# Vision tower on one core: ScalarE issues the image loads, gray stores and gathers, and the rows of maxima go in one transfer

## What is computed

```python
gray = jnp.einsum('bchw,c->bhw', x, w)[:, None]
edges = jax.lax.conv_general_dilated(gray, scharr, (1, 1), 'SAME', ...)
edge = jnp.sqrt(jnp.square(edges)).sum(axis=1) / 2
h = concatenate([cls_tok, edge], axis=1)          # 257 tokens
h = h + attention(layernorm(h))                   # softmax, causal
h = h + ffn(layernorm(h))                         # quantised input, weights and product
```

## Time and profile before

| | us |
|---|---|
| median of 3 runs | 1346.86 (1345.83 to 1353.33) |
| the profiled execution | 1357.62 |
| its span from the first to the last instruction | 1355.9 |
| TensorE busy in it | 1036.2 (76%) |
| VectorE busy | 857.1 (63%) |
| ScalarE busy | 685.5 (51%) |
| GpSimd busy | 537.8 (40%) |

### The profile page before, as it was taken

The page is one execution under the profiler, slowest core; times in us unless marked ns, Lnnn a source line. Parts: engine busy times, 40 slices in busy tenths (PEclk is TensorE's granted clock), DMA queues, the critical chain, the costliest instruction groups (busy, mean ns, idle before and its releaser), DMA issues. The chain is left out here.

```text
span 1355.9 us, 28643 instructions
## 1 busy us (share of the span) xinstructions
PE 1036.2 (76%) x9565; PEld 711.0 (52%) x9574; DVE 857.1 (63%) x1987; ACT 685.5 (51%) x1171; POOL 537.8 (40%) x645
## 2 busy tenths in 40 slices
PE   2458888888898988988898898887743766636665
PEld 1236666666666666666666666666532333313332
DVE  2134656667666676666676755664555888888664
ACT  1235555556555555655565555544223676633332
POOL 4244554465555555555555554543210000003222
PEclk9978989899999899999999988987766999976656
DMA  3565445555455554554565544423200334401764
GB/s 102 142 136 143 109 113 126 131 128 150 111 141 132 131 131 124 150 136 127 126 147 130 135 120 109 106 61 101 68 10 1 128 138 160 170 1 48 234 233 160
DMA packets 158498, 164.38 MB, mean 121 GB/s; under 512 B 29384, under 2 KB 153196, under 8 KB 155372
## 3 DMA queue, kind: packets, MB, share of 16 engines
q1 hardware_dynamic: 158444, 163.68, 44.4%
HBM read 73.26 MB, written 34.12 MB: 79 GB/s over the span
## 5 line engine op out<-in xcount | busy, mean ns | idle before, releaser
L519 ACT ACTIVATE prob<-ST 128x772 f32<-128x772 f32 x256 | 209.6, 819 | 218.3 <-PE ST L929 215.1
L684 DVE TENSOR_REDUCE mneg<-SX 128x2 f32<-128x258 f32 x256 | 107.6, 420 | 313.6 <-PE SX L915 313.1
L912 PE MATMUL SX<-kst,qst 96*128 96x257 bf16 (+1 forms) x1024 | 168.7, 259 | 44.1 <-DMA qst<-qpart 39.4
L929 PE MATMUL ST<-qst,kst 98*128 98x256 bf16 (+2 forms) x1536 | 145.5, 229 | 45.5 <-DMA qst<-mpart 45.0
L686 DVE TENSOR_REDUCE mneg<-SX 128x2 f32<-128x514 f32 x256 | 173.9, 679 | 0.0
L929 PEld LDWEIGHTS ST<-qst,kst 98*128 98x128 bf16 x1536 | 124.6, 102 | 69.3 <-DMA qst<-mpart 32.8
L915 PE MATMUL SX<-mask_s,ident_b 128*128 128x256 bf16 x512 | 148.2, 290 | 0.0
L912 PEld LDWEIGHTS SX<-kst,qst 96*128 96x128 bf16 x1024 | 97.1, 102 | 90.0 <-issue 64.3
L445 POOL TENSOR_SCALAR_AFFINE_SELECT prob<-prob 128x1016 f32<-128x1016 f32 x128 | 142.3, 1112 | 0.0
L1512 PE MATMUL GU<-qst,hq 128*128 128x256 bf16 (+1 forms) x384 | 87.2, 379 | 49.1 <-ACT hq L1303 49.1
L948 PE MATMUL G<-prob,vaug 128*32 128x256 f32 (+2 forms) x3072 | 118.9, 285 | 2.6 <-POOL prob L445 2.5
(11 more groups left out here) (228 smaller groups left out, 2106.0 us busy)
## 6 DMA issues: line engine op xcount, KB each, us to landing
kst<-kpart SPq DMA_DIRECT2D x192, 128.5 KB, 2.5
gst<-gray_dram SPq DMA_DIRECT2D x96, 256.0 KB
qst<-qpart SPq DMA_DIRECT2D x192, 128.0 KB, 2.4
h_dram<-hb SPq DMA_DIRECT2D x12, 1280.0 KB, 4.6
hb<-h_dram SPq DMA_DIRECT2D x12, 1280.0 KB, 6.1
wg_raw<-in_x SPq DMA_DIRECT2D x48, 256.0 KB, 4.0
wu_raw<-in_x SPq DMA_DIRECT2D x48, 256.0 KB, 4.1
gray_dram<-gray SPq DMA_DIRECT2D x64, 128.0 KB, 2.8
```

The source lines that it names most:

```text
L519: nc.scalar.activation(prob[:, g % 2, 2 * (u % 2):2 * (u % 2) + 2, 0:QEND], ST[:, :, 0:QEND], ACT.Exp).then_inc(exp_done, 1)
L684: nc.vector.tensor_reduce(mneg[:, 0, u // 4, 0, at], SX[:, :, S0:S0 + P + 1], AX.X, ALU.max, negate=True)
L912: mm(SX[:, r, at:at + k], qst[par][0:SR, 2 * u + r, P * t:P * t + P], kst[par][0:SR, 2 * u + r, 0:k], start=t == 1, stop=False)
L929: last = mm(ST[0:KEYS[k], r, QAT[k]:QAT[k] + QN[k]], kst[par_][:, i, KFIRST[k]:KFIRST[k] + KEYS[k]], qst[par_][:, i, Q0[k]:IMG], start=Tru ...
```

## The change

Five things change, all in the attention block:

1. `load_x`, the gray store and the gathers leave SP for ScalarE. `images()` (loads of image n+1, then the store of `bW`) stands behind the exponential of unit 5 of `bT`. `gathers(0, GR, 0)`, the three large gathers, stands behind the exponential of unit 7 of `bT`, and `gathers(GR, 2, 3 * GR)`, the three small ones, behind that of unit 1 of `bS`. The same bytes are moved by the same number of transfers (11 per image). The load of image 0 stays on SP.
2. `max_rows` issues one transfer of 2 x 8 x 256 in place of two of 1 x 8 x 256; the waits for `m_loaded` follow.
3. On VectorE `split(bS, 0)` stands before `edge_stats(bC)`, not behind it.
4. On SP the wait for `sT_done` stands before the `vlast` transfer, which now waits for `max_done` and no longer for `v_last` and `pv_done`.
5. On SP the wait for `rec_spread` ahead of `rec` is left out.

```diff
             def max_rows(b, par, half_):
 
                 if valid(b):
                     wait(sp, msplit, b, 2, half_ + 1)
-                    for i in range(2):
-                        sp.dma_start(qst[par][SR + i:SR + i + 1, 8 * half_:8 * half_ + 8, :],
-                                     mpart[half_][8 * i:8 * i + 8, :]).then_inc(m_loaded[half_], 16)
+                    sp.dma_start(qst[par][SR:SR + 2, 8 * half_:8 * half_ + 8, :], mpart[half_][:, :]
+                                 ).then_inc(m_loaded[half_], 16)
...
                     wait(sp, rec_done, bO, 1, 1)
-                    wait(sp, rec_spread, bO - 1, 1, 1)
                     sp.dma_start(rec[:, :], den[:, :]).then_inc(rec_moved, 16)
-                if valid(bW):
-                    wait(sp, gray_step, bW, 2, 2)
-                    wait(sp, gst_loaded, bC, 96, 96)
-                    for t in range(QT):
-                        sp.dma_start(gray_dram[1 + P * t:1 + P * t + P, 1:1 + IMG],
-                                     gray[:, t, :]).then_inc(gray_saved, 16)
-                if valid(n + 1):
-                    wait(sp, gray_step, bW, 2, 2)
-                    load_x(n + 1, odd)
-                if valid(bW):
-                    wait(sp, gray_saved, bW, 32, 32)
-                    wait(sp, conv_done, bC, 2, 2)
-                    for dx in range(3):
-                        for row, k, at in ((0, GR, GR * dx), (GR, 2, 3 * GR + 2 * dx)):
...
                 max_rows(bS, par, 0)
+                wait(sp, sT_done, bT, 8, 8)
                 if valid(bS):
-                    wait(sp, v_last, bS, 1, 1)
-                    wait(sp, pv_done, bT - 1, 4, 4)
+                    wait(sp, max_done, bS, 8, 4)
...
                 if valid(bP):
-                    wait(sp, sT_done, bT, 8, 8)
                     wait(sp, k_low, bP, 1, 1)
...
+                def images():
+
+                    if valid(n + 1):
+                        wait(act, gray_step, bW, 2, 2)
+                        load_x(n + 1, odd)
+                    if valid(bW):
+                        wait(act, gray_step, bW, 2, 2)
+                        wait(act, gst_loaded, bC, 96, 96)
+                        for t in range(QT):
+                            act.dma_start(gray_dram[1 + P * t:1 + P * t + P, 1:1 + IMG],
+                                          gray[:, t, :]).then_inc(gray_saved, 16)
+
+                def gathers(row, k, first):
+
+                    if valid(bW):
+                        wait(act, gray_saved, bW, 32, 32)
+                        wait(act, conv_done, bC, 2, 2)
+                        for dx in range(3):
+                            at = first + k * dx
+                            src = bass.AP(gray_dram.tensor, dx + row * (IMG + 2),
+                                          [[IMG + 2, k], [GR * (IMG + 2), GB], [1, IMG]])
+                            act.dma_start(gst[at:at + k, :, :], src).then_inc(gst_loaded, 16)
...
                 exponential(bT, 5)
+                images()
                 queries(0)
...
                 exponential(bT, 7)
+                gathers(0, GR, 0)
...
                 exponential(bS, 1)
+                gathers(GR, 2, 3 * GR)
...
                 edge_tile(bC, 1)
+                split(bS, 0)
                 edge_stats(bC)
-                split(bS, 0)
                 maxima(bS, 4)
```

More of the change, by code:

```diff
@@ L288, in vit_tower @@
         block = attention.enter_context(nc.Block())
+        xv = x.rearrange("b c (t p) w -> b p c t w", p=P)
         @block.sync
@@ L332, in _ @@
             sp.wait_ge(s_zero, 16 * 8)
[L333 to L340, removed]
+            for c in range(CH):
+                sp.dma_start(xin[0][:, c, :, :], xv[0][:, c]).then_inc(x_loaded[0], 16)
             def max_rows(b, par, half_):
@@ L360, in step @@
                     wait(sp, rec_done, bO, 1, 1)
-                    wait(sp, rec_spread, bO - 1, 1, 1)
                     sp.dma_start(rec[:, :], den[:, :]).then_inc(rec_moved, 16)
-                if valid(bW):
-                    wait(sp, gray_step, bW, 2, 2)
-                    wait(sp, gst_loaded, bC, 96, 96)
-                    for t in range(QT):
-                        sp.dma_start(gray_dram[1 + P * t:1 + P * t + P, 1:1 + IMG],
-                                     gray[:, t, :]).then_inc(gray_saved, 16)
-                if valid(n + 1):
-                    wait(sp, gray_step, bW, 2, 2)
-                    load_x(n + 1, odd)
-                if valid(bW):
-                    wait(sp, gray_saved, bW, 32, 32)
-                    wait(sp, conv_done, bC, 2, 2)
-                    for dx in range(3):
-                        for row, k, at in ((0, GR, GR * dx), (GR, 2, 3 * GR + 2 * dx)):
-                            src = bass.AP(gray_dram.tensor, dx + row * (IMG + 2),
-                                          [[IMG + 2, k], [GR * (IMG + 2), GB], [1, IMG]])
-                            sp.dma_start(gst[at:at + k, :, :], src).then_inc(gst_loaded, 16)
                 max_rows(bS, par, 0)
+                wait(sp, sT_done, bT, 8, 8)
                 if valid(bS):
-                    wait(sp, v_last, bS, 1, 1)
-                    wait(sp, pv_done, bT - 1, 4, 4)
+                    wait(sp, max_done, bS, 8, 4)
                     sp.dma_start(vaug[par][KW - 1:KW, KT - 1, :, 0:HD], vlast[:, :].rearrange("p (h d) -> p h d", d=HD)
@@ L505, in _, with load_x @@
             act.wait_ge(s_prep, 11)
+            def load_x(b, par):
+                src = xv[b] if isinstance(b, int) else xv[bass.ds(b, 1)].rearrange("o p c t w -> (o p) c t w")
+                for c in range(CH):
+                    act.dma_start(xin[par][:, c, :, :], src[:, c]).then_inc(x_loaded[par], 16)
             def step(n, par):
-                bC, bP, bS, bT = n - 2, n - 3, n - 4, n - 5
+                bW, bC, bP, bS, bT = n - 1, n - 2, n - 3, n - 4, n - 5
+                odd = 1 - par
+                def images():
[17 more added lines that the diff above has]
+                            act.dma_start(gst[at:at + k, :, :], src).then_inc(gst_loaded, 16)
                 def exponential(b, u):
@@ L699, in split @@
                     wait(dve, mT_done, b, 2, half_ + 1)
-                    wait(dve, m_loaded[half_], b - 1, 32, 32)
+                    wait(dve, m_loaded[half_], b - 1, 16, 16)
                     nc.vector.tensor_copy(mpart[half_][:, :], M[1][0:H, 0:IMG]).then_inc(msplit, 1)
@@ L924, in scores_t @@
                         if u % 4 == 0:
-                            wait(pe, m_loaded[u // 4], b, 32, 32)
+                            wait(pe, m_loaded[u // 4], b, 16, 16)
                         for r in range(2):
```

## The result

| | us |
|---|---|
| median before, 4 runs | 1346.34 (1341.0 to 1353.33) |
| median after, 4 runs | 1436.33 (1429.3 to 1440.69) |
| ratio | 1.066, 95% interval 1.0595 to 1.0725 |
| the profiled execution of after | 1429.3 (span 1427.6) |

Slower by 90 us, 33 above the forecast and inside the range. The table of stretches of the changed kernel first (columns as in the earlier trace rows): 200 to 800 us, which answers to the earlier trace rows; the 8 us behind a `scores(0)` at 604.09 and those behind one at 237.20; the 10 us in which gathers, `kst` and `qst` move together; and five single microseconds of that meeting and of its end.

The account below looks back on a forecast made before the run. Bound: a per-image ring through TensorE, VectorE, SP and DMA. Terms -0.4 - 0.7 - 0.2 + 2.9 + 0.45 = +2.05 us per image; 28 x 2.0 = 56; 1357.6 + 56, less 10.8: 1403 us, range 1318 to 1439.

Parts of the forecast that it names:

- The landing: Last `qst` issue to `scores(0)`: late gathers meet `kst` and `qst` on the DMA engines, +2.9 us per image.
- image 0: The old trace's one meeting of gathers and `kst`: 4.81 us to `scores(0)` instead of 1.93, 193 GB/s at share 1.16.
- rival A: DMA queues fill each other's gaps, rate rising to 300 GB/s: 1311 us, or 1330 with a remainder; chance 0.25.
- B: Gains and losses cancel, `qst` landing 1.0 to 1.5 us later: 1340 to 1354 us; chance 0.12.
- The other signs: Profile after: `qst<-qpart` wait 80 us or more, `qst<-mpart` below 25, `kst` within some 1.5 us of the first gather.
- The split, the one transfer, `rec`: VectorE's earlier split, one transfer for the maxima, `rec` leaving earlier: -0.4, -0.7 and -0.2 us per image.
- Issuing: Eleven issues moved from SP to ScalarE: nothing gained on SP, zero cost taken on ScalarE, 0.5 us kept for the range.
- Rival C: SP held at each ScalarE issue, its bursts exceeding 3.84 us: about +1.3 us more per image, 1439 us; chance 0.13.
- a sign against itself: TensorE's waits for exponentials appearing where it had none would show the forecast wrong on ScalarE.
- The clock: TensorE idle about 3 us before each `scores(0)`: every image, not about half, pays 0.9 us, +0.45 us per image.
- the 28 images: Images 1 to 28 or so meet the new overlap: 28 x 2.0 = 56 us; nothing taken for head and tail.
- the ring: Each image's chain: about 15.7 us from `scores(0)` to SP's rows of maxima, then 12 us of SP and DMA.

Follow-up runs that it names:

- e5: Changed kernel with each gather moving one of its eight blocks, same issues, places and engines: 1300.56 us.
- e7: Kernel before with parts 2 to 5 of the change, SP issuing all, its six gathers moved between `vlast` and `kst`: 1474.03 us.
- e10: Changed kernel with twenty useless products on TensorE in the wait for the stacked queries: 1361.36 us.
- e11: Kernel before with six useless products on TensorE in the wait for the stacked queries: 1328.58 us.
- e1: Changed kernel with ScalarE's loads, store and gathers issued earlier, some 3 us further ahead of `kst`: 1341.93 us.
- e2: Kernel before with parts 2 to 5 of the change, SP still issuing loads, store and gathers: 1292.15 us.
- e3: Changed kernel with two transfers for the rows of maxima and the split behind the statistics, as before: 1408.48 us.

## Why the prediction was right, and what it mis-sized

**The landing: right.** 1.98 became 4.68, +2.70 for the +2.9 that image 0 had shown. The share in the meeting (1.11) is like image 0's 1.16, the rate is higher, 228 for 193 GB/s, but far from rival A's 300. e5 shows that it is the bytes, e7 that two queues are not the cause. Rivals A and B are out. The other signs came as well: TensorE's wait for `qst<-qpart` 90.6 us, that for `qst<-mpart` 13.0, `kst` 1.05 us behind the first gather.

**The split, the one transfer, `rec`: right and a little small.** Together 1.3 us were forecast. With the clock held up in both kernels (e10 against e11) `mpart` to `kst` fell by 0.77 and `scores(0)` to `mpart` by 0.79, 1.56 us. The waits for `rec` went but for the one of 12.8, as said.

**Issuing: right.** Nothing for SP, next to nothing for ScalarE (0.13 us by e5). e1 shows that this holds for the places and not for ScalarE as such. TensorE's waits for POOL's part of the exponentials grew from 2.5 to 30.1 us, which the prediction had named as a sign against itself. But this wait took the place of the one for `mpart` (45.0 to 13.0): e2 has 9.9 and 27.2 us, e5 29.8 and 10.3, and e5 still runs at 1301 us.

**Rival C: wrong by its own test.** SP's bursts took 3.88 and 3.92 us, before 3.84 and 3.83. It is ScalarE's issues that got longer, 1.69 for 1.32 us. The Trainium skill, "Perfetto Trace Analysis", section "DMA Instruction — HWDGE (DVE, Sync)", has a descriptor generator, shared by the sequencers of VectorE and SyncE, that is locked for each transfer; 0.06 us per burst of six leave little of this for SP, and only the longer issues of ScalarE would fit it. That the median came out at C's 1439 is no support for C.

**The clock: the term that was mis-sized.** Right in kind, far too small: +0.45 us per image forecast, about 2.0 measured. e10 against after: the changed kernel loses 2.75 us per image to the clock. e11 against before: that one loses 0.73. The difference is 2.02 (1.82, if the 0.20 us of landing in e11 are left out). I had priced a full loss at 0.9 us, from two images of the kernel before whose wait was 0.87 to 0.91 us and whose 8 us were at 0.79 or 1.00, and assumed that a wait of 3 us would only bring that same loss at every image. But behind 2.8 us the clock is about 0.61 for those 8 us, at every image from 266 to 800 us. With every term as measured the sum is -0.79 - 0.77 + 0.08 + 2.49 + 2.02 = +3.03 us (the landing from 2.18 in e11 to 4.67 in e10).

**Some of the nearness is luck.** The clock alone was 1.57 us per image too small. The other terms together came out 0.6 us per image better than forecast (+1.0 measured, +1.6 forecast), which hid part of it. The result lies above the 1380 to 1420 us of the forecast proper; it is the bound that rival C gave that holds it. And the 28 images are not seen in the two traces: there 21 periods carry the loss, and 8.8 us lie ahead of image 0's `scores(0)`, where the prediction took nothing.

By the medians, filling the wait gives 75 us back in the changed kernel and 19 in the one before. So of the 90 us about 56 are the clock, and about 34 the ring and the head. The chances for A and B (0.37) rested on rows that could be read either way; image 0 was the better witness.

**Best version.** e2 at 1292 us: the small edits without the move to ScalarE.

**Open.** Why 2.45 us idle in the middle of an image (e3) brought 0.79 for the next 8 us, while 2.73 us ahead of `scores(0)` brought 0.61: the amount of work before and after differs too, and no run separates the two. Nor is the length of the wait all: the two images of the changed kernel at 207 and 237 us waited 3.36 and 2.98 us and had 0.79. That filling would help e2 further wasn't tried.

## What to carry over

When a transfer is moved to another engine's queue, first ask at what time it will now move, and what else the same DMA engines carry then; a lone burst that is paced by its issues (0.72 share, 199 GB/s) has little room to spare (228 GB/s at 1.11 was all that came out of it). Price a longer wait of TensorE as the wait plus what the granted clock loses behind it, and take that from a stretch with a wait of the new length, not of the old. Where the wait can't be removed, throwaway products in it may be worth more than they look.

## What was not expected of the hardware

- 2.36 us of useless products per image made the changed kernel 75 us faster, and 0.8 us of them made the kernel before 19 us faster.
- In the kernel before, a wait of 0.87 us was followed by a granted clock of 0.79 over 8 us (559.33) and one of 0.91 us by 1.00 (586.96). Behind about 2.8 us it was 0.59 to 0.64 at most images, and behind 4.2 us down to 0.50 at nine of nineteen.
- Short-row copies inside SBUF ran alone at 199 GB/s with a share of 0.72; together with the gathers and a backlog it was 228 GB/s at 1.11. The share rose by half, the rate by 15%.
